# Edge counting: GpSimd forms the node one-hot of every second edge tile

## The chip, the core and the metric

The kernel runs on one core of one Trainium2 chip. The core has TensorE (matrix products and transposes, results in PSUM), VectorE, ScalarE and GpSimd (elementwise engines), and SyncE, which issues most transfers. Each engine works through its own queue in order; engines wait for each other by semaphores. The metric is the time on the device in microseconds (us), median of the runs.

## The reference, cut to what matters

Four layers on 1250 nodes of 512 features; the source and target node of the 41250 edges come as two integer lists, sorted by target.

```python
edge_index = jnp.stack([src, dst])
deg = jnp.maximum(segment_sum(ones(dst.shape), dst, num_segments=1250), 1.0)
x = x + _L0_gnn_ref(_layernorm(x), L0_gnn_wc, L0_gnn_wn, L0_gnn_bias, edge_index)
x = x + _L0_ffn_ref(_layernorm(x)[None], ...)[0]
x = x + _L1_gnn_ref(_layernorm(x), src, dst, deg, ...)
x = x + _L1_ffn_ref(_layernorm(x)[None], ...)[0]
# in _L0_gnn_ref
sums = segment_sum(beta[dst], src, num_segments=x.shape[0])
# in _L1_gnn_ref
neigh_sum = segment_sum(x[edge_src], edge_dst, num_segments=n)
```

The kernel does not gather rows. It first counts the edges into a dense matrix of 1280 by 1280 numbers (and its transpose), how many edges lead from node s to node d, and both graph layers multiply by it. The change is in that counting, `count_edges`.

## The kernel before, in words

The program is a row of stages, each with its own semaphores and a barrier at its end: loading constants (`load_consts`), `count_edges`, the first graph layer, causal attention with the experts, the second graph layer, and the top-16 attention layer.

`count_edges` takes the edges in tiles of 128, ET = 323 of them. Edge e lies on partition e of its tile. A source node s is split into a block `s >> 7` (0 to 9) and a place in the block `s & 127`. For each tile two one-hot matrices are formed, each by one `tensor_scalar` that compares `m.ruler` (0, 1, 2, ... in f16) with a number of its own on each partition (a column of `ends`, f32):

- `hot_b` (128 columns): a one at the source's place in its block;
- `hot_m` (320 columns): a one at (target less the first target of the tile's window) x 10 + block. Since the edges are sorted by target, a tile's targets lie in a window of 32.

TensorE multiplies `hot_b` (as the weights it loads) by `hot_m`, which adds the tile's 128 edges to the counts in PSUM. The counts lie in 25 chunks of 51 targets; a tile whose window crosses a chunk's edge takes two matmuls (`spans`). Four PSUM banks take the chunks in turn. TensorE opens a bank with a product by zero (L327), closes it with another (L330), ScalarE copies it to `m.AT` (L396), and after every third or so chunk TensorE flips a block of 128 targets by ten transposes (L336), which ScalarE writes to `m.A` (L400).

Both one-hots have a ring of HOTS = 8 buffers. In the loop of VectorE (L319 to L322) tile t waits, from t = 8 on, until TensorE has used tile t - 8 (`s_used`), then writes `hot_b` (L305) and `hot_m` (L306); the second counts `s_onehot` up. TensorE waits for `s_onehot` at t + 1 (L376), loads and multiplies (L378) and counts `s_used` up (L382). GpSimd has two small instructions at the stage's start (L256, L257) and then stands at the barrier. The order of each queue is that of the code.

There is a second way through the stage (L310 to L317 and L355 to L368), for edges whose targets do not fit the windows. It is chosen by a flag from the data; with these inputs it is not taken.

Later stages that the prediction reads: `node_rows` (L404 to L428), in which VectorE casts each row block to f16 (`hi`, L422) and GpSimd forms the rest (`lo`, L428), and the causal attention, in which VectorE and GpSimd both scale softmax rows by a number on each partition: VectorE `ex_big` (L1006), GpSimd `ex_small` (L742). In that stage GpSimd also splits keys and queries (L725 to L735).

Of the kernel before, what the change touches and what calls it, by code (L numbers as in the profile page):

```python
# [16 lines left out]
ALU = mybir.AluOpType  # L17
# [3 lines left out]
P = 128  # L21
N = 1250
NT = (N + P - 1) // P
# [8 lines left out]
ET = (NE + P - 1) // P  # L32
EG = (ET + P - 1) // P
HOTS = 8
CD = 51
CHUNKS = 4
WIN = 32
# [150 lines left out]
def window(t):  # L188

    return min(max((t * SLOPE >> 6) - REACH, 0), N - WIN)  # L190


def count_edges(nc, m, io, ahead):
# [4 lines left out]
    def spans(t):  # L198

        lo, hi = window(t), window(t) + WIN  # L200
        return [(c, max(lo, c * CD), min(hi, (c + 1) * CD)) for c in range(lo // CD, (hi - 1) // CD + 1)]
# [7 lines left out]
    def whole(c):  # L209

        return [j for j in range(NT) if c == min((min((j + 1) * P, N) - 1) // CD, NC - 1)]

    with ExitStack() as ctx:
        s = Stage(nc, m, ctx, "ce")
        (s_blank, s_edges, s_tiles, s_base, s_split, s_flag, s_turned, s_cols, s_lined, s_flagged, s_onehot, s_used,
         s_closed, s_drained, s_flipped, s_kept, s_shift) = s.signals(
            "blank edges tiles base split flag turned cols lined flagged onehot used closed drained flipped kept "
            "shift")
        raw = s.sb("raw", [P, 2, EG, P], I32)
        part = s.sb("part", [P, 2, EG, P], I32)  # L220
# [1 line left out]
        ends = s.sb("ends", [P, 3, EG * P])  # L222
        hot_b = s.sb("hot_b", [P, HOTS, P], F16)
# [3 lines left out]
        base = s.sb("base", [P, EG])  # L227
        worst = s.sb("worst", [P, 3])
        flag = s.sb("flag", [1, 2])
# [24 lines left out]
        @block.gpsimd  # L254
        def _(pool):
            pool.iota(tile_i[:, :], [[P, EG]], base=0, channel_multiplier=1).then_inc(s_tiles, 1)  # L256
            pool.memset(m.AT[:, :, NC * CD:NP], 0.0).then_inc(s_tiles, 1)  # L257

        @block.vector
        def _(dve):  # L260
            dve.memset(raw[:, 0, :, :], AWAY).then_inc(s_blank, 1)
            dve.memset(raw[:, 1, :, :], N - 1).then_inc(s_blank, 1)
            dve.memset(none[:, :], 0.0).then_inc(s_blank, 1)

            dve.wait_ge(s_tiles, 1)
            dve.tensor_scalar(tile_i[:, :], tile_i[:, :], SLOPE, None, ALU.mult).then_inc(s_base, 1)
            dve.wait_ge(s_base, 1)
            dve.tensor_scalar(tile_i[:, :], tile_i[:, :], 6, None, ALU.arith_shift_right).then_inc(s_base, 1)
            dve.wait_ge(s_base, 2)
            dve.tensor_scalar(base[:, :], tile_i[:, :], float(-REACH), 0.0, ALU.add, ALU.max).then_inc(s_base, 1)  # L270
            dve.wait_ge(s_base, 3)
            dve.tensor_scalar(base[:, :], base[:, :], float(N - WIN), None, ALU.min).then_inc(s_base, 1)

            dve.wait_ge(s_edges, 16 * 2 * (EG + 1))
            dve.tensor_scalar(part[:, 0, :, :], raw[:, 0, :, :], P - 1, None, ALU.bitwise_and).then_inc(s_split, 1)
            dve.tensor_scalar(part[:, 1, :, :], raw[:, 0, :, :], 7, None, ALU.arith_shift_right).then_inc(s_split, 1)
            dve.wait_ge(s_base, 4)
            dve.tensor_tensor(key[:, 3, :, :], raw[:, 1, :, :], base[:, :].unsqueeze(2).broadcast_to([P, EG, P]),
                              ALU.subtract).then_inc(s_split, 1)
            dve.wait_ge(s_split, 3)  # L280
            dve.tensor_copy(key[:, 0, :, :], part[:, 0, :, :]).then_inc(s_split, 1)
            dve.scalar_tensor_tensor(out=key[:, 1, :, :], in0=key[:, 3, :, :], scalar=float(NT), in1=part[:, 1, :, :],
                                     op0=ALU.mult, op1=ALU.add).then_inc(s_split, 1)
            dve.scalar_tensor_tensor(out=key[:, 2, :, :], in0=raw[:, 1, :, :], scalar=float(NT), in1=part[:, 1, :, :],
                                     op0=ALU.mult, op1=ALU.add).then_inc(s_split, 1)

            drel = key[:, 3, :, :].rearrange("p g e -> p (g e)")
            dve.tensor_reduce(worst[:, 0:1], drel, AX_X, ALU.max).then_inc(s_flag, 1)
            dve.tensor_reduce(worst[:, 1:2], drel, AX_X, ALU.min, negate=True).then_inc(s_flag, 1)
            dve.wait_ge(s_flag, 2)  # L290
            dve.scalar_tensor_tensor(out=worst[:, 2:3], in0=worst[:, 0:1], scalar=float(1 - WIN), in1=worst[:, 1:2],
                                     op0=ALU.add, op1=ALU.max).then_inc(s_flag, 1)
            dve.wait_ge(s_lined, 1)
            dve.tensor_reduce(flag[:, 0:1], ps_w[:, 0:P], AX_X, ALU.max).then_inc(s_flag, 1)
            dve.wait_ge(s_flag, 4)
            dve.tensor_scalar(flag[:, 1:2], flag[:, 0:1], 0.0, None, ALU.is_gt).then_inc(s_flag, 1)
            dve.wait_ge(s_flag, 5)
            dve.tensor_copy(flag_i[:, :], flag[:, 1:2]).then_inc(s_flagged, 1)
            dve.wait_ge(s_turned, 1)
            dve.tensor_copy(ends[:, :, :].rearrange("p n e -> p (n e)"), ps_f[:, 0:3 * EG * P]).then_inc(s_cols, 1)  # L300
            dve.wait_ge(s_cols, 1)
            dve.wait_ge(s_flagged, 1)

            def one_hot(u, b_of, m_of, width):
                dve.tensor_scalar(hot_b[:, u, :], m.ruler[:, 0:P], b_of, None, ALU.is_equal)  # L305
                dve.tensor_scalar(hot_m[:, u, 0:width], m.ruler[:, 0:width], m_of, None, ALU.is_equal  # L306
                                  ).then_inc(s_onehot, 1)

            scattered = dve.value_load(flag_i[0:1, 0:1], min_val=0, max_val=1)
            with dve.If(scattered):  # L310
                with dve.Fori(0, NC) as c:
                    with dve.Fori(0, ET) as t:
                        dve.wait_ge(s_used, c * ET + t + 1)
                        one_hot(0, ends[:, 0, bass.ds(t, 1)], ends[:, 2, bass.ds(t, 1)], CW)
                    dve.wait_ge(s_used, c * ET + ET + 1)
                    dve.tensor_scalar(ends[:, 2, :], ends[:, 2, :], float(-CW), None, ALU.add).then_inc(s_shift, 1)
                    dve.wait_ge(s_shift, c + 1)  # L317
            with dve.Else():
                for t in range(ET):  # L319
                    if t >= HOTS:  # L320
                        dve.wait_ge(s_used, t - HOTS + 2)
                    one_hot(t % HOTS, ends[:, 0, t:t + 1], ends[:, 1, t:t + 1], WIN * NT)  # L322

        @block.tensor
        def _(pe):
            def open_chunk(bank):
                pe.matmul(bank[:, 0:CW], none[:, :], m.ruler[:, 0:CW], start=True, stop=False)  # L327

            def close_chunk(bank):
                pe.matmul(bank[:, 0:CW], none[:, :], m.ruler[:, 0:CW], start=False, stop=True).then_inc(s_closed, 1)  # L330
# [38 lines left out]
            with pe.Else():  # L369
                for t in range(ET):  # L370
                    for c, lo, hi in spans(t):
                        if opens[c] == t:
                            if c >= CHUNKS:
                                pe.wait_ge(s_drained, c - CHUNKS + 1)
                            open_chunk(ps_c[:, c % CHUNKS, :])
                    pe.wait_ge(s_onehot, t + 1)  # L376
                    for c, lo, hi in spans(t):
                        mm = pe.matmul(ps_c[:, c % CHUNKS, (lo - c * CD) * NT:(hi - c * CD) * NT],  # L378
                                       hot_b[:, t % HOTS, :],
                                       hot_m[:, t % HOTS, (lo - window(t)) * NT:(hi - window(t)) * NT],  # L380
                                       start=False, stop=False)
                    mm.then_inc(s_used, 1)  # L382
                    for c, lo, hi in spans(t):
                        if closes[c] == t:
                            close_chunk(ps_c[:, c % CHUNKS, :])
                    for c in range(NC):
                        if closes[c] == t - LATER or (t == ET - 1 and t - LATER < closes[c]):
                            for j in whole(c):
                                pe.wait_ge(s_drained, c + 1)
                                flip(j)  # L390
# [1888 lines left out]
```

## Time and profile before

| | |
|---|---|
| median of 3 runs | 1774.48 us (1774.18 to 1774.99) |
| profiled execution's own time | 1774.77 us |
| its span | 1772.1 us |
| TensorE busy | 1527.8 us (86%) |
| VectorE busy | 1062.0 us (60%) |
| GpSimd busy | 525.6 us (30%) |
| edge tiles 8 to 322, on the timeline | 43.15 to 161.35 us |

The times in the trace are microseconds from the start of the span, in one profiled execution. In the rows PE is TensorE's matmuls, PEld its weight loads, DVE is VectorE, ACT ScalarE, POOL GpSimd, SPq SyncE's queue. An instruction's duration runs from its start to its end; on one engine the next may start before it ends, so the sum of durations can be more than the time that passed. A row of the timeline that ends in x3 merges three instructions in a row.

### The profile page before, as it was taken

The numbers are of one execution on the slowest core, as the hardware profiler recorded it, in microseconds if no ns is written. First come the engines' busy times: TensorE is split into PE (matmuls) and PEld (weight loads), VectorE is DVE, ScalarE is ACT, GpSimd is POOL, SyncE is SP. The second block draws the span as 40 slices with busy tenths as digits, with TensorE's granted clock in tenths as the row PEclk, the third lists the DMA queues.
The fourth block names the chain that finished last, engine by engine and source line by source line (L and its number), as shares of the span: only waits on it lengthen the run. The fifth ranks groups of instructions, "written<-read, shape, count | busy, mean of one in ns | idle before, by whom it ended". The sixth has DMA issues, their size and how long they took to land. (4 is left out here: it accounts for less than half of the span.)

```text
span 1772.1 us, 22747 instructions
## 1 busy us (share of the span) xinstructions
PE 1527.8 (86%) x8385; PEld 940.5 (53%) x8385; DVE 1062.0 (60%) x2052; ACT 699.6 (39%) x1333; POOL 525.6 (30%) x388
## 2 busy tenths in 40 slices
PE   1885888789787788999999989958898999998878
PEld 0332544344466665445454654535586676776654
DVE  4998433333478774111322331574999999999991
ACT  0224000133365554110111132042778778878771
POOL 0001100000456651000000006001876766676550
PEclk9998899899899999999999999989999999999999
DMA  6000100000622212300000020002011011111001
GB/s 220 1 1 1 74 0 0 0 1 1 179 60 43 48 31 86 132 0 0 1 0 0 1 72 0 0 1 60 1 31 31 1 31 31 23 32 31 1 1 58
DMA packets 28570, 56.99 MB, mean 32 GB/s; under 512 B 7904, under 2 KB 12644, under 8 KB 28208
## 3 DMA queue, kind: packets, MB, share of 16 engines
q1 hardware_dynamic: 27600, 54.01, 11.0%
q10 hardware_dynamic: 864, 1.57, 0.3%
q8 instruction: 66, 1.08, 0.3%
q14 instruction: 40, 0.33, 0.1%
HBM read 28.77 MB, written 5.84 MB: 20 GB/s over the span
## 5 line engine op out<-in xcount | busy, mean ns | idle before, releaser
L1431 POOL TENSOR_TENSOR tl_ex<-tl_ex,tl_left 128x1250 f32<-128x1250 f32 x80 | 209.8, 2622 | 37.3 <-ACT tl_left L1733 33.2
L1552 PE MATMUL tl_banks<-identf,tl_ex 128*128 128x128 f32 x800 | 139.4, 290 | 42.2 <-ACT tl_pt L1754 25.7
L1272 DVE SCALAR_TENSOR_TENSOR X<-ex_ps_x,g,X 128x512 f32<-128x512 f32 x80 | 59.9, 750 | 192.6 <-PE ex_ps_x L1165 192.6
L1138 PE MATMUL ex_ps_h<-yt,w 128*128 128x512 f32 (+1 forms) x384 | 144.5, 531 | 0.0
L1165 PE MATMUL ex_ps_x<-w,hid 128*128 128x512 f32 (+1 forms) x320 | 143.1, 599 | 0.0
L1552 PEld LDWEIGHTS tl_banks<-identf,tl_ex 128*128 128x128 f32 x800 | 90.0, 144 | 97.4 <-ACT tl_pt L1754 44.4
L1754 ACT COPY tl_pt<-tl_banks 128x512 f32<-128x512 f32 (+1 forms) x200 | 108.4, 542 | 83.5 <-PE tl_banks L1552 79.7
L1218 ACT ACTIVATE hid<-ex_ps_h,b 128x512 f32<-128x512 f32 (+1 forms) x48 | 29.2, 610 | 242.6 <-PE ex_ps_h L1138 242.6
L1829 DVE MAX8 tl_m<-tl_banks 128x8 f32<-128x1250 f32 x80 | 116.3, 1454 | 5.6 <-PE tl_banks L1529 5.6
L1733 ACT ACTIVATE tl_left<-tl_left,tl_negm 128x1250 f32<-128x1250 f32 x80 | 107.6, 1345 | 29.0 <-DVE tl_left L1837 28.6
L1835 DVE MAX8 tl_m<-tl_left 128x8 f32<-128x1250 f32 x80 | 117.1, 1464 | 2.8
L1905 POOL TENSOR_TENSOR lo<-xn,hi 128x512 f16<-128x512 f32 x5 | 5.9, 1188 | 379.7 <-ACT hi L1995 379.7
L1833 DVE MATCH_REPLACE8 tl_left<-tl_m,tl_banks 128x1250 f32<-128x1250 f32 x80 | 116.0, 1450 | 0.0
L1837 DVE MATCH_REPLACE8 tl_left<-tl_m,tl_left 128x1250 f32<-128x1250 f32 x80 | 115.6, 1445 | 0.0
L378 PE MATMUL ce_ps_c<-ce_hot_m,ce_hot_b 128*128 128x320 f16 (+29 forms) x518 | 98.2, 261 | 14.5
L1138 PEld LDWEIGHTS ex_ps_h<-yt,w 128*128 128x128 f32 x384 | 74.8, 196 | 66.2 <-issue 66.0
L1727 ACT ACTIVATE tl_ex<-tl_banks,tl_negm 128x1250 f32<-128x1250 f32 x80 | 104.9, 1311 | 2.4 <-DVE tl_left L1833 1.3
L1567 PE MATMUL tl_banks<-tl_pt,tl_V 128*64 128x128 f32 x1600 | 104.8, 278 | 0.0
L1165 PEld LDWEIGHTS ex_ps_x<-w,hid 128*128 128x128 f32 (+1 forms) x320 | 60.3, 189 | 73.9 <-issue 73.9
L306 DVE TENSOR_SCALAR ce_hot_m<-ruler,ce_ends 128x320 f16<-128x320 f16 x323 | 96.5, 299 | 0.0
L1567 PEld LDWEIGHTS tl_banks<-tl_pt,tl_V 128*64 128x64 f32 x1600 | 85.7, 137 | 14.2 <-issue 14.2
L1486 PE MATMUL tl_banks<-tl_ct,tl_wt 128*128 128x512 f32 (+1 forms) x192 | 82.0, 554 | 9.2 <-DVE tl_ct L1804 6.2
(268 smaller groups left out, 2963.8 us busy)
## 6 DMA issues: line engine op xcount, KB each, us to landing
kl<-KT SPq DMA_DIRECT2D x16, 320.0 KB, 4.4
qs<-QO SPq DMA_DIRECT2D x16, 320.0 KB, 5.8
tl_kl<-tl_KT SPq DMA_DIRECT2D x16, 320.0 KB, 4.4
tl_qs<-tl_QO SPq DMA_DIRECT2D x16, 320.0 KB, 6.0
w<-in_L_ffn_W SPq DMA_DIRECT2D x8, 512.0 KB
w<-in_L_ffn_W SPq DMA_DIRECT2D x4, 1024.0 KB, 9.8
at_kept<-AT SPq DMA_DIRECT2D x1, 3200.0 KB, 9.0
AT<-at_kept SPq DMA_DIRECT2D x1, 3200.0 KB, 18.9
```

What stands on the lines that cost most here:

```text
L1138: mm = pe.matmul(h_bank(u)[:, 0:w], w1[e][:, k, j * P:(j + 1) * P], yt[:, G % 2, k, 0:w], start=(k == 0), stop=(k == KD - 1))
L1165: mm = pe.matmul(x_bank(v)[0:rows(t), :], hid[:, (EX * G + e) % HIDS, j, r * P:r * P + rows(t)], w2[:, 2 * e + j, :], start=(j == 0), stop ...
L1431: pool.tensor_tensor(ex[:, n % EXS, 0:N], ex[:, n % EXS, 0:N], left[:, n % LEFT, :], ALU.subtract).then_inc(s_probs, 1)
L1552: mm = pe.transpose(ps_t[:, b * P:(b + 1) * P], ex[:, n % EXS, a + b * P:a + (b + 1) * P], m.identf[:, :])
L1567: mm = pe.matmul(ps_o[u * DH:(u + 1) * DH, 0:P], V[:, h // 2 % 2, k, h % 2 * DH:(h % 2 + 1) * DH], pt[:, (2 * j + u) % PTS, k * P:(k + 1) ...
L1727: act.activation(ex[:, n % EXS, 0:N], logits(n)[:, 0:N], ACT.Exp, bias=negm[:, n:n + 1]).then_inc(s_exp, 1)
L1733: act.activation(lf, lf, ACT.Exp, bias=negm[:, n:n + 1]).then_inc(s_rest, 1)
L1754: act.copy(pt[:, n % PTS, a:a + w], ps_t[:, 0:w]).then_inc(s_kept, 1)
L1829: dve.max(m8[:, n % TOPS, 0:8], logits(n)[:, 0:N]).then_inc(s_max, 1)
L1833: dve.match_replace(lf, m8[:, n % TOPS, 0:8], logits(n)[:, 0:N], TAKEN).then_inc(s_read, 1)
L1835: dve.max(m8[:, n % TOPS, 8:16], lf).then_inc(s_max2, 1)
L1837: dve.match_replace(lf, m8[:, n % TOPS, 8:16], lf, TAKEN).then_inc(s_topped, 1)
```

## The change

In the windowed way, GpSimd forms `hot_b` of the odd tiles (1, 3, ..., 321: 161 of them), with the same comparison. It starts when `ends` is there (`s_cols`), waits from tile 9 on for TensorE's use of tile t - 8, as VectorE does, and counts a semaphore of its own up, `s_half_hot`. VectorE forms `hot_b` of even tiles only, and `hot_m` of all. TensorE waits at odd tiles for `s_half_hot` too.

```diff
@@ gpsimd
             pool.memset(m.AT[:, :, NC * CD:NP], 0.0).then_inc(s_tiles, 1)
+            pool.wait_ge(s_cols, 1)
+            for t in range(1, ET, 2):
+                if t >= HOTS:
+                    pool.wait_ge(s_used, t - HOTS + 2)
+                pool.tensor_scalar(hot_b[:, t % HOTS, :], m.ruler[:, 0:P], ends[:, 0, t:t + 1], None, ALU.is_equal
+                                   ).then_inc(s_half_hot, 1)
@@ vector
             def one_hot(u, b_of, m_of, width):
-                dve.tensor_scalar(hot_b[:, u, :], m.ruler[:, 0:P], b_of, None, ALU.is_equal)
+                if b_of is not None:
+                    dve.tensor_scalar(hot_b[:, u, :], m.ruler[:, 0:P], b_of, None, ALU.is_equal)
                 dve.tensor_scalar(hot_m[:, u, 0:width], m.ruler[:, 0:width], m_of, None, ALU.is_equal
                                   ).then_inc(s_onehot, 1)
@@
-                    one_hot(t % HOTS, ends[:, 0, t:t + 1], ends[:, 1, t:t + 1], WIN * NT)
+                    one_hot(t % HOTS, None if t % 2 else ends[:, 0, t:t + 1], ends[:, 1, t:t + 1], WIN * NT)
@@ tensor
                     pe.wait_ge(s_onehot, t + 1)
+                    if t % 2:
+                        pe.wait_ge(s_half_hot, t // 2 + 1)
                     for c, lo, hi in spans(t):
```

VectorE's queue where the ring of eight is full for the first time, tiles 7 to 9, before:

```order
L305 TENSOR_SCALAR ce_hot_b<-ruler,ce_ends 128x128
L306 TENSOR_SCALAR ce_hot_m<-ruler,ce_ends 128x320
L305 TENSOR_SCALAR ce_hot_b<-ruler,ce_ends 128x128 [waits ce2_used]
L306 TENSOR_SCALAR ce_hot_m<-ruler,ce_ends 128x320
L305 TENSOR_SCALAR ce_hot_b<-ruler,ce_ends 128x128 [waits ce2_used]
L306 TENSOR_SCALAR ce_hot_m<-ruler,ce_ends 128x320
```

The same place in the changed kernel, tiles 6 to 9 (its lines stand seven further down):

```order
L312 TENSOR_SCALAR ce_hot_b<-ruler,ce_ends 128x128
L313 TENSOR_SCALAR ce_hot_m<-ruler,ce_ends 128x320 x2
L312 TENSOR_SCALAR ce_hot_b<-ruler,ce_ends 128x128 [waits ce2_used]
L313 TENSOR_SCALAR ce_hot_m<-ruler,ce_ends 128x320
L313 TENSOR_SCALAR ce_hot_m<-ruler,ce_ends 128x320 [waits ce2_used]
```

The `hot_b` of tiles 7 and 9 are gone from VectorE's queue, and the wait on `s_used` of tile 9 is now that of its `hot_m`. GpSimd's queue from the stage's start to the next stages, before:

```order
L256 IOTA ce_tile_i 128x3
L257 MEMSET AT 128x10x5
L213 UNCONDITIONAL_BRANCH
L75 ISA [waits barrier_Pool_Activation_PE_DVE_SP_gather] x2
L424 UNCONDITIONAL_BRANCH
L428 TENSOR_TENSOR gp_lo<-gl_xn,gp_hi 128x512 [waits ce2_edges] x10
```

And in the changed kernel:

```order
L256 IOTA ce_tile_i 128x3
L257 MEMSET AT 128x10x5
L262 TENSOR_SCALAR ce_hot_b<-ruler,ce_ends 128x128 [waits ce2_cols]
L262 TENSOR_SCALAR ce_hot_b<-ruler,ce_ends 128x128 x3
L262 TENSOR_SCALAR ce_hot_b<-ruler,ce_ends 128x128 [waits ce2_used] x157
L213 UNCONDITIONAL_BRANCH
```

161 instructions stand between GpSimd's small ones and the stage's end, 157 of them behind a wait on `s_used`.

## Rows read from the trace of the kernel before

**Rows 1.** The page: span, then busy time and share of each engine.

```profile
span 1772.1 us, 22747 instructions
PE 1527.8 (86%) x8385; PEld 940.5 (53%) x8385; DVE 1062.0 (60%) x2052; ACT 699.6 (39%) x1333; POOL 525.6 (30%) x388
```

**Rows 2.** Table of stretches, tiles 8 to 322: busy us (x instructions), TensorE clock, DMA.

```profile
core 0: us, PE busy (x) PEld busy (x) DVE busy (x) ACT busy (x) POOL busy (x), PEclk, DMA share, GB/s
43.15:161.35 118.20, 103.76 (x652) 42.27 (x650) 118.20 (x630) 25.62 (x41) 0.00 (x0) 1.00 0.01 1
```

**Rows 3.** Waits, 43.1 to 161.4: total us, times, longest.

```profile
PEld ce_ps_c L378 <- DVE ce_hot_m L306: 73.9, 283, 0.3
...
DVE ce_hot_b L305 <- PE ce_ps_c L378: 3.9, 1, 3.9
```

**Rows 4.** Groups by line of VectorE (busy us, mean ns), then timeline (start, us).

```profile
L306 DVE TENSOR_SCALAR ce_hot_m<-ruler,ce_ends 128x320 f16<-128x320 f16 x315 | 94.1, 299 | 0.0
L305 DVE TENSOR_SCALAR ce_hot_b<-ruler,ce_ends 128x128 f16<-128x128 f16 x315 | 78.6, 250 | 3.9 <-PE ce_ps_c L378 3.9
...
50.29 0.25 DVE L305 TENSOR_SCALAR ce_hot_b<-ruler,ce_ends 128x128 f16<-128x128 f16 x1
...
50.45 0.30 DVE L306 TENSOR_SCALAR ce_hot_m<-ruler,ce_ends 128x320 f16<-128x320 f16 x1
50.66 0.25 DVE L305 TENSOR_SCALAR ce_hot_b<-ruler,ce_ends 128x128 f16<-128x128 f16 x1
```

**Rows 5.** Timeline of the stage's start, VectorE and TensorE.

```profile
36.16 0.25 DVE L305 TENSOR_SCALAR ce_hot_b<-ruler,ce_ends 128x128 f16<-128x128 f16 x1 [1.19 <-issue]
...
42.24 0.60 PE L327 MATMUL ce_ps_c<-ruler,ce_none 128*128 128x510 f16 x1 [7.06 <-issue]
...
42.64 2.60 PE L378 MATMUL ce_ps_c<-ce_hot_m,ce_hot_b 128*128 128x320 f16 x9
...
43.15 0.26 DVE L305 TENSOR_SCALAR ce_hot_b<-ruler,ce_ends 128x128 f16<-128x128 f16 x1 [3.90 <-PE ce_ps_c L378]
```

**Rows 6.** Timeline of TensorE around a flip.

```profile
122.19 0.60 PEld L336 LDWEIGHTS ce_ps_f<-ident,AT 128*128 128x128 f16 x10
...
122.75 0.19 PEld L378 LDWEIGHTS ce_ps_c<-ce_hot_m,ce_hot_b 128*128 128x128 f16 x2
...
123.22 0.17 PEld L378 LDWEIGHTS ce_ps_c<-ce_hot_m,ce_hot_b 128*128 128x128 f16 x2 [0.18 <-DVE ce_hot_m L306]
```

**Rows 7.** Groups by line of GpSimd, whole span: busy us, mean ns.

```profile
L742 POOL TENSOR_SCALAR ex_small<-ex_small,inv 128x128 f32<-128x128 f32 x8 | 4.8, 605 | 41.9 <-DVE inv L1001 41.9
L742 POOL TENSOR_SCALAR ex_small<-ex_small,inv 128x256 f32<-128x256 f32 x8 | 7.4, 923 | 6.4 <-DVE inv L1001 5.4 <-POOL kl L727 1.0
L742 POOL TENSOR_SCALAR ex_small<-ex_small,inv 128x640 f32<-128x640 f32 x8 | 15.1, 1883 | 20.1 <-DVE inv L1001 20.1
L1425 POOL TENSOR_SCALAR tl_negm<-tl_m 128x1 f32<-128x1 f32 x80 | 16.8, 210 | 118.0 <-DVE tl_m L1829 101.5 <-ACT tl_left L1733 14.7
L1409 POOL CAST tl_kh<-tl_kl 128x1280 fp32r<-128x1280 f32 x7 | 8.8, 1251 | 0.5
L126 POOL TENSOR_SCALAR_AFFINE_SELECT identf<-identf 128x128 f32<-128x128 f32 x1 | 0.3, 292 | 0.2 <-POOL ld_ruler_i L124 0.2
```

**Rows 8.** Timeline of `node_rows`: VectorE's casts and GpSimd's subtractions, single instructions.

```profile
169.05 0.43 DVE L422 CAST gp_hi<-gl_xn 128x512 f16<-128x512 f32 x1 [1.45 <-ACT gl_xn L415]
169.57 1.15 POOL L428 TENSOR_TENSOR gp_lo<-gl_xn,gp_hi 128x512 f16<-128x512 f32 x1 [146.21 <-DVE gp_hi L422]
170.93 0.41 DVE L422 CAST gp_hi<-gl_xn 128x512 f16<-128x512 f32 x1
172.31 1.34 POOL L428 TENSOR_TENSOR gp_lo<-gl_xn,gp_hi 128x512 f16<-128x512 f32 x1
172.56 1.38 DVE L422 CAST gp_hi<-gl_xn 128x512 f16<-128x512 f32 x1
173.61 1.33 POOL L428 TENSOR_TENSOR gp_lo<-gl_xn,gp_hi 128x512 f16<-128x512 f32 x1
173.85 1.37 DVE L422 CAST gp_hi<-gl_xn 128x512 f16<-128x512 f32 x1
174.90 1.33 POOL L428 TENSOR_TENSOR gp_lo<-gl_xn,gp_hi 128x512 f16<-128x512 f32 x1
```

**Rows 9.** Timeline of causal attention: VectorE's L1006 and GpSimd's instructions beside it.

```profile
468.82 0.87 DVE L1006 TENSOR_SCALAR ex_big<-ex_big,inv 128x1250 f32<-128x1250 f32 x1
473.09 0.62 POOL L742 TENSOR_SCALAR ex_small<-ex_small,inv 128x128 f32<-128x128 f32 x1 [9.26 <-DVE inv L1001]
473.78 1.25 POOL L725 CAST kh<-kl 128x1280 fp32r<-128x1280 f32 x1
474.40 1.24 DVE L1006 TENSOR_SCALAR ex_big<-ex_big,inv 128x1152 f32<-128x1152 f32 x1
479.94 1.25 POOL L730 CAST qh<-qs 64x1280 fp32r<-64x1280 f32 x1
480.16 1.57 DVE L1006 TENSOR_SCALAR ex_big<-ex_big,inv 128x1024 f32<-128x1024 f32 x1
```

More of the change, by code:

```diff
@@ L214, in count_edges @@
         s = Stage(nc, m, ctx, "ce")
-        (s_blank, s_edges, s_tiles, s_base, s_split, s_flag, s_turned, s_cols, s_lined, s_flagged, s_onehot, s_used,
+        (s_blank, s_edges, s_tiles, s_base, s_split, s_flag, s_turned, s_cols, s_lined, s_flagged, s_onehot, s_half_hot, s_used,
          s_closed, s_drained, s_flipped, s_kept, s_shift) = s.signals(
-            "blank edges tiles base split flag turned cols lined flagged onehot used closed drained flipped kept "
+            "blank edges tiles base split flag turned cols lined flagged onehot half_hot used closed drained flipped kept "
             "shift")
```

## The prediction

> **What bounds the kernel now.** The page says that VectorE is busy 60% of the span and GpSimd 30%, and that the profiled execution's span is 1772.1 us; its own time is 1774.77 us, so 2.7 us lie around the span, and the median of the three runs shown is 1774.48 us, 0.3 us below it [rows 1]. The shares are averages; the change touches one stage, so I read that stage alone. The table of stretches from 43.15 to 161.35 us has VectorE busy all 118.20 us with 630 instructions, GpSimd at 0.00 and TensorE's granted clock at 1.00, its upper level of 2.4 GHz [rows 2]. The view of waits over the same stretch says who is late: TensorE's weight load waits for `ce_hot_m` 283 times, 73.9 us in all, while VectorE waits once, 3.9 us, and that just ahead of the stretch [rows 3]. VectorE sets the pace and TensorE follows tile by tile.
>
> The 630 instructions are 315 tiles (8 to 322) of two each, so a tile costs 118.20 / 315 = 0.375 us. That is less than the sum of the durations, 0.250 + 0.299 us: the timeline has the start of `hot_m` 0.16 us after that of `hot_b`, and the next `hot_b` starts 0.21 to 0.22 us after `hot_m`, before `hot_m` has ended [rows 4]. What an instruction costs VectorE in this row is the spacing, not the duration: 0.163 us for `hot_b`, 0.212 for `hot_m`. The first eight tiles are outside this: VectorE builds them from 36.16 us on, in 3 us, and TensorE cannot take the first before 42.24 us [rows 5]. After the last tile comes a tail of banks, copies and a flip that does not change, and then a stage boundary. Nothing else runs beside this stage for later use except loads that are over by about 44 us, so each us more or less here is one at the end.
>
> **How much room TensorE has.** It waits 73.9 of 118.2 us, which leaves (118.2 - 73.9) / 315 = 0.14 us of its own per tile. After ten transposes (0.60 us) it takes up two tiles with 0.19 us of loads between them, opens a bank and is back to waiting at 123.22 us [rows 6]. TensorE is no bound at any pace discussed here; even at its lower clock level, where I double all of it, it would want 0.28 us of the tile. The new wait of TensorE on `s_half_hot` at odd tiles stands just behind one on `s_onehot` and costs nothing as long as GpSimd is ahead; behind it are only that tile's matmuls.
>
> **Removed.** 161 instructions `hot_b` leave VectorE; 4 of them belong to the first eight tiles and are hidden behind TensorE's late start, 157 count (tiles 9, 11, ..., 321). Each gives back its spacing: 157 x 0.163 = -25.6 us. A pair of tiles then costs VectorE 0.750 - 0.163 = 0.587 us. Nothing else is late before that: TensorE needs 0.28 us a pair.
>
> **Added: GpSimd's own pace.** GpSimd runs 161 `TENSOR_SCALAR` of 128x128 f16 with a per-partition scalar. The trace has no such instruction in f16. The nearest is the softmax scaling at L742, the same operation, 128x128 in f32 with a per-partition scalar: 605 ns. From there to 640 columns (1883 ns) it grows by 1278 / 512 = 2.50 ns a column, and with one column it takes 210 ns (L1425). Lower bound: the rate of GpSimd's CAST, 1251 ns for 1280 columns, or 0.98 ns a column: 210 + 127 x 0.98 = 335 ns. Upper bound: the same operation at twice the columns, 923 ns, in case the comparison or the 16-bit type doubles the work of a column [rows 7]. I take 605 ns, since operation, shape and the kind of scalar agree and only type and comparison do not. Two instructions of GpSimd in a row leave about 0.07 us between them (0.62 us from 473.09, the next at 473.78 [rows 9]). So GpSimd alone would need 0.675 us for each pair, less than the 0.750 of now. GpSimd's waits on `s_used` come true eight tiles ahead of need, and nothing else is in its queue until the stage ends.
>
> The Trainium skill, in "GPSIMD Engine Reference", section "4.1 Engine selection", calls one-input work on GpSimd roughly line rate. The row of L742 disagrees at 2.50 ns a column, the row of CAST is close to it; the sum by that rule is that of the first rival below.
>
> **Added: what GpSimd does to VectorE.** This decides. The stage has never had both engines at work, but two later ones have. In the stage that splits the node rows, VectorE casts 128x512 f32 to f16 while GpSimd subtracts. With GpSimd idle the cast takes 0.43 or 0.41 us; beside GpSimd it takes 1.37 to 1.38. It ends about 0.29 us after GpSimd's instruction has ended (172.31 + 1.34 = 173.65; 172.56 + 1.38 = 173.94) and GpSimd's next one takes 1.33 us instead of 1.15. One of each goes by every 1.30 us (172.31, 173.61, 174.90) [rows 8]. They exclude each other and take turns. A second place shows it for the very kind of instruction at stake: VectorE's `TENSOR_SCALAR` with a per-partition scalar (L1006) takes 0.87 us for 1250 columns with GpSimd idle; beside a GpSimd CAST that runs until 475.03 us, 1152 columns take 1.24 us and end 0.61 us after it; beside one until 481.19, 1024 columns take 1.57 us and end 0.54 us after it [rows 9]. Both are 0.53 ns a column with no start left over, so the instruction stood ready and its data moved only once GpSimd was done.
>
> Does that hold for `hot_b` and `hot_m`? From 128 to 320 columns they grow by 299 - 250 = 49 ns, 0.26 ns a column [rows 4], twice the rate of the blocked L1006, so I expect them to want at least as much of what is shared. The Trainium skill says it outright in "SBUF — State Buffer", section "Who interferes with whom": VectorE's copies, casts and tensor_scalars in the two-port modes, of which the four-a-cycle one is the fastest, and GpSimd lock each other out for a whole instruction. By that rule the trace agrees for the casts and L1006 [rows 8, 9]; no row here shows it for f16 on both sides.
>
> The price of one GpSimd instruction to VectorE: GpSimd hides some of its start. Of a 1.30 us turn 0.29 is VectorE's, so GpSimd keeps the way for 1.01 of the 1.15 us that it takes alone, 0.14 less [rows 8]. For ours: 0.605 - 0.14 = 0.46 us. VectorE's next instruction has its own start behind it by then: alone 1152 columns would take about 0.82 us (0.87 less 98 columns of 0.53 ns), and after the release they took 0.61, so 0.21 is hidden [rows 9]; the cast hid 0.41 - 0.29 = 0.12 [rows 8]. A `hot_m` of 0.30 us then ends 0.09 to 0.18 us after the release, where it would have ended 0.21 us after its forerunner. Price: 0.46 + 0.09 - 0.21 = 0.34 us, or 0.43 with the cast's figure. I take 0.34, as L1006 is the same operation.
>
> **Sum.** A pair goes from 0.750 to 0.587 + 0.34 = 0.927 us. 157 x 0.34 = +53.4, less 25.6, is +27.8 us. Against the profiled execution 1774.8 + 27.8 = 1802.6, against the median **1802.3 us**. The rest (157 waits on GpSimd, 161 on TensorE) is in queues that have slack: 0.
>
> **Rivals.**
> (1) *The short instruction*, faster. GpSimd forms the one-hot at its CAST's rate, 0.335 us. It keeps the way 0.195 us, the price is 0.195 + 0.09 - 0.21 = 0.075 and the net -0.088 us a pair: 157 x -0.088 = -13.8, 1760.7 us. The point from which it decides is a price of 0.163, that is an instruction of about 0.42 us (0.163 + 0.21 - 0.09 + 0.14). For it: CAST and AFFINE_SELECT (292 ns for 128x128). Against it: all eight L742 of 128x128 average 605 [rows 7]. Chance 0.09, and 0.04 for a length close to the point, within 0.2%.
> (2) *No exclusion* at this rate. Then GpSimd's own 0.675 us is the pair: -0.075 x 157 = -11.8, 1762.7 us. Against it rows 8 and 9. Chance 0.05.
> (3) *The long instruction*: 0.923 us. It keeps the way 0.78, the price is 0.66 and the net +0.50: +78, 1852.6 us. Chance 0.12.
> (4) *VectorE keeps GpSimd out* until it has run eight tiles ahead and stalls on `s_used`; then four GpSimd instructions run alone (2.7 us) after VectorE's burst (2.35), with a hand-over through TensorE of some 0.5 us each way (its first matmul starts at 42.64, VectorE resumes at 43.15 [rows 5]): 6.05 us for four pairs, 1.51 a pair, +119 us, 1894 us. Against it: the turns of rows 8, where GpSimd got its turn although VectorE's next cast was already waiting. Chance 0.04.
>
> **How the numbers follow.** My own case (a price between 0.20 and 0.60) has 0.66. About 0.2% or 3.5 us is what a measurement of this kernel can tell from no change. Faster is (1) and (2), 0.14; same 0.04; slower 0.66 + 0.12 + 0.04 = 0.82. The range goes from 1770, under the low prices, to 1853, case (3); it leaves out (1), (2) and (4), 0.18.
>
> **What would show it.** In the changed profile: GpSimd's new line of 161 instructions at 0.6 to 0.75 us; `hot_m` no longer all at 0.299 us, but one in two or three near 0.6 to 0.75 us; the stage 28 us longer (about 0.93 us from one GpSimd instruction to the next); TensorE still waiting for `ce_hot_m`, or for `ce_hot_b` of GpSimd; all later stages the same length. I am wrong in the price if the instructions on GpSimd last under 0.42 us, in the exclusion if `hot_m` keeps its 0.299 us, and in the turns if GpSimd's instructions come in clusters of four.

## The result, and the profile after

The changed kernel takes 1768.0 us (median of 15 runs, 1762.67 to 1773.66), the kernel before 1775.32 us in the same rounds (15 runs, 1772.44 to 1780.06). The ratio is 0.9953 with a 95% interval of 0.9941 to 0.9965: 7 to 8 us, or 0.5%, faster. Timed again on another occasion the ratio was 0.9965 (0.9948 to 0.9982). The forecast was 28 us slower. One execution of a version further down is left out of its ratio: it ran at a granted clock of 0.558 instead of about 0.96 and took 2600.35 us.

The page of the changed kernel, against [rows 1]: the span is 6.7 us shorter, VectorE has 161 instructions fewer, GpSimd 161 more and 113 us more of work.

```profile
span 1765.4 us, 22908 instructions
PE 1508.5 (85%) x8385; PEld 943.1 (53%) x8385; DVE 1054.9 (60%) x1891; ACT 698.9 (40%) x1333; POOL 638.8 (36%) x549
```

The table of stretches of the changed kernel (busy us and instructions of TensorE, its weight loads, VectorE, ScalarE and GpSimd, then TensorE's clock) for 157 pairs of tiles in the loop, against [rows 2]; then the same kernel's groups by line of VectorE and GpSimd there, against [rows 4, 7]:

```profile
42.67:153.24 110.57, 82.30 (x648) 42.89 (x646) 110.57 (x471) 25.60 (x41) 110.48 (x157) 1.00 0.01 1
...
L313 DVE TENSOR_SCALAR ce_hot_m<-ruler,ce_ends 128x320 f16<-128x320 f16 x314 | 95.2, 343 | 0.0
L312 DVE TENSOR_SCALAR ce_hot_b<-ruler,ce_ends 128x128 f16<-128x128 f16 x157 | 42.8, 272 | 0.0
...
L262 POOL TENSOR_SCALAR ce_hot_b<-ruler,ce_ends 128x128 f16<-128x128 f16 x157 | 110.7, 724 | 6.0 <-PE ce_ps_c L387 6.0
```

VectorE's 471 instructions are 157 x 3. A pair takes 110.57 / 157 = 0.704 us, where it took 0.750. Both engines are busy all the time, and `hot_m` has grown from 299 to 343 ns on average. The waits of the same kernel, from 43 to 160 us, against [rows 3]:

```profile
PEld ce_ps_c L387 <- DVE ce_hot_m L313: 58.6, 134, 0.6
PE ce_ps_c L387 <- DVE ce_hot_m L313: 21.2, 64, 0.4
...
PE ce_ps_c L387 <- POOL ce_hot_b L262: 0.6, 4, 0.2
```

TensorE still waits for the one-hots, as forecast, and has time to spare. VectorE's last `hot_m` ends at 153.24 us, before at 161.43, 8.2 us earlier; 7.1 of it is the loop (118.1 us from the `hot_m` of tile 8 on before, 111.0 now) and 1.1 is that TensorE began a little earlier in this execution. The rest of the program took 1610.67 us before and 1612.16 us now, in which nothing was changed; 1.5 us is well within what runs of one kernel differ by.

So VectorE gave back what was forecast and GpSimd took less than forecast. Of 0.587 us a pair without `hot_b`, 0.704 - 0.587 = **0.117 us** is the price of one GpSimd instruction, where the prediction had 0.34 and the point that decides lay at 0.163.

The timeline shows the price instruction by instruction (start, duration, both in us). First the stage's beginning, where GpSimd was not held up, then the steady loop, in which the pattern repeats every two pairs:

```profile
34.01 2.39 POOL L262 TENSOR_SCALAR ce_hot_b<-ruler,ce_ends 128x128 f16<-128x128 f16 x4 [11.68 <-DVE ce_ends L306]
...
35.80 0.60 POOL L262 TENSOR_SCALAR ce_hot_b<-ruler,ce_ends 128x128 f16<-128x128 f16 x1
...
35.84 0.37 DVE L312 TENSOR_SCALAR ce_hot_b<-ruler,ce_ends 128x128 f16<-128x128 f16 x1
36.13 0.37 DVE L313 TENSOR_SCALAR ce_hot_m<-ruler,ce_ends 128x320 f16<-128x320 f16 x1
...
80.38 0.85 POOL L262 TENSOR_SCALAR ce_hot_b<-ruler,ce_ends 128x128 f16<-128x128 f16 x1
...
80.76 0.27 DVE L312 TENSOR_SCALAR ce_hot_b<-ruler,ce_ends 128x128 f16<-128x128 f16 x1
80.95 0.37 DVE L313 TENSOR_SCALAR ce_hot_m<-ruler,ce_ends 128x320 f16<-128x320 f16 x1
...
81.20 0.60 POOL L262 TENSOR_SCALAR ce_hot_b<-ruler,ce_ends 128x128 f16<-128x128 f16 x1
81.24 0.42 DVE L313 TENSOR_SCALAR ce_hot_m<-ruler,ce_ends 128x320 f16<-128x320 f16 x1
...
81.78 0.85 POOL L262 TENSOR_SCALAR ce_hot_b<-ruler,ce_ends 128x128 f16<-128x128 f16 x1
```

Undisturbed, GpSimd's instruction lasts 0.60 us, the 605 ns that was taken from L742, and four of them in a row take 2.39 us, 0.60 each with nothing between them. In the loop every second one lasts 0.85: there GpSimd is held up and VectorE runs its pair in its own 0.59 us. Beside the end of that one and the next, of 0.60, VectorE is held up, and its two `hot_m` last 0.37 and 0.42. VectorE starts its pairs at 80.17, 80.76, 81.58, 82.17: 0.59, 0.82, 0.59. The rows from 35.80 on already contradict the forecast's picture: a `hot_b` ends at 36.21 while GpSimd is busy until 36.40. VectorE is held up, but not until GpSimd is done.

### The profile page after: what moved, and what is told of

Same layout as the page of the kernel before. It is cut to its first block and busy times, and to the rows that moved or that the text cites. A ratio compares the mean times of both kernels' runs of the same rounds, so it can differ in the third digit from the quotient of the medians.

```text
span 1765.4 us, 22908 instructions
## 1 busy us (share of the span) xinstructions
PE 1508.5 (85%) x8385; PEld 943.1 (53%) x8385; DVE 1054.9 (60%) x1891; ACT 698.9 (40%) x1333; POOL 638.8 (36%) x549
## 3 DMA queue, kind: packets, MB, share of 16 engines
q10 hardware_dynamic: 864, 1.57, 0.3%
## 5 line engine op out<-in xcount | busy, mean ns | idle before, releaser
L262 POOL TENSOR_SCALAR ce_hot_b<-ruler,ce_ends 128x128 f16<-128x128 f16 x161 | 113.1, 722 | 17.7 <-DVE ce_ends L306 11.7
L387 PE MATMUL ce_ps_c<-ce_hot_m,ce_hot_b 128*128 128x320 f16 (+29 forms) x518 | 75.0, 252 | 28.3 <-DVE ce_hot_m L313 21.2
```

The source lines that it names most:

```text
L262: pool.tensor_scalar(hot_b[:, t % HOTS, :], m.ruler[:, 0:P], ends[:, 0, t:t + 1], None, ALU.is_equal).then_inc(s_half_hot, 1)
```

## The experiments

Two theories of the price were put against each other. **W**, the prediction's: GpSimd keeps VectorE out for its whole duration less 0.14 us. **P**: it keeps VectorE out only during a part of its instruction. The measure throughout is the loop, from VectorE's start on the `hot_m` of tile 8 to the end of its last `hot_m`: 118.1 us in the kernel before. The loops are read from one profiled execution of each kernel.

### Spare instructions on GpSimd beside an unchanged VectorE

Four kernels add to the kernel before a row of comparisons on GpSimd into a buffer that nobody reads. VectorE's work is that of before, so the loop's growth over their number is the price. The first of them:

```diff
+            pool.wait_ge(s_cols, 1)
+            pool.wait_ge(s_used, 16)
+            for i in range(140):
+                if i >= 4:
+                    pool.wait_ge(s_idle, i - 3)
+                pool.tensor_scalar(spare[:, i % 4, :], m.ruler[:, 0:P], ends[:, 0, i:i + 1], None, ALU.is_equal
+                                   ).then_inc(s_idle, 1)
```

The others have f32 input and output (x2), 50 instructions of 512 columns in f16 (x3), and 50 of 512 in f32 (x4).

> The kernel before, with 140 more instructions on GpSimd beside VectorE's one-hot loop: the same comparison, 128x128 f16 with a per-partition scalar, into a spare buffer nobody reads, from tile 16 on. VectorE's own work is untouched, so the lengthening of the loop divided by 140 is the price of one such instruction to VectorE. Theory W (the prediction's: GpSimd keeps VectorE out for its whole duration less 0.14 us): 0.34 us each, the loop 48 us longer. Theory P (it keeps the shared way for only a part of its duration): 0.10 to 0.20 us each, 14 to 28 us longer.

> The same with f32 input and output, 128x128. Theory W: 0.34 us each, 48 us in all, as in f16. Theory P, if the part that GpSimd holds goes by bytes: twice the price of the f16 run, 0.2 to 0.4 us. Theory P, if it goes by columns or instructions: the price of the f16 run.

> 50 spare GpSimd instructions of 128x512 f16 instead of 140 of 128x128. At 2.5 ns a column one lasts 1.56 us. Theory W: 1.56 - 0.14 - 0.12 = 1.3 us each, the loop 65 us longer, and no hot_m or hot_b ends in the middle of a GpSimd instruction. Theory P: VectorE's instructions go on ending while GpSimd's runs; the price is 0.2 to 0.6 us, 10 to 30 us in all.

> The same 50 with f32 input and output, 128x512, which is the very form of L742 beside L1006 in the attention stage, where L1006 ended only after GpSimd had. Theory W: 65 us longer. Theory P with a part that goes by bytes: twice the f16 run. If this one shows full exclusion and the f16 one does not, the type decides; if neither does, the length of VectorE's instructions decides (short ones slip in between).

| spare instructions | loop, us | price, us | mean duration on GpSimd |
|---|---|---|---|
| 140 of 128 columns, f16 | 136.2 | 18.1 / 140 = 0.13 | 0.874 |
| 140 of 128 columns, f32 | 152.3 | 34.2 / 140 = 0.24 | 0.639 |
| 50 of 512 columns, f16 | 157.6 | 39.5 / 50 = 0.79 | 1.576 |
| 50 of 512 columns, f32 | 157.5 | 39.4 / 50 = 0.79 | 1.574 |

W had 0.34 and 1.3: it falls in all four. The 512-column run shows why. Groups by line of GpSimd in that run, then its timeline:

```profile
L264 POOL TENSOR_SCALAR ce_spare<-ruler,ce_ends 128x512 f16<-128x512 f16 x50 | 77.8, 1576 | 23.3 <-PE ce_ps_c L385 23.3
...
79.91 1.56 POOL L264 TENSOR_SCALAR ce_spare<-ruler,ce_ends 128x512 f16<-128x512 f16 x1
79.95 0.69 DVE L312 TENSOR_SCALAR ce_hot_b<-ruler,ce_ends 128x128 f16<-128x128 f16 x1
80.56 0.29 DVE L313 TENSOR_SCALAR ce_hot_m<-ruler,ce_ends 128x320 f16<-128x320 f16 x1
80.77 0.24 DVE L312 TENSOR_SCALAR ce_hot_b<-ruler,ce_ends 128x128 f16<-128x128 f16 x1
80.94 0.64 DVE L313 TENSOR_SCALAR ce_hot_m<-ruler,ce_ends 128x320 f16<-128x320 f16 x1
81.46 1.57 POOL L264 TENSOR_SCALAR ce_spare<-ruler,ce_ends 128x512 f16<-128x512 f16 x1
```

Beside one GpSimd instruction of 1.56 us VectorE runs four. The first is lengthened by 0.44 us (0.69 against 0.25), the next two not at all, the fourth by 0.34 (0.64 against 0.30). GpSimd's comparison shuts VectorE out twice, once in its first half and once before its end, and leaves it alone between. The two stretches make up 0.79 of 1.57 us. P holds. P's size for 512 columns (0.2 to 0.6) was too low. Bytes do not matter at 512 columns, where f16 and f32 cost the same. That run's expectation had said that, if neither type showed full exclusion, the length of VectorE's instructions would decide. The copy below, beside the same short instructions, and two rows of the kernel before, shown with the account of the prediction, speak against it: the operation on GpSimd matters, and where in it VectorE's instruction falls.

At 128 columns f32 costs twice f16, but bytes alone are not the reason: with f32, GpSimd lasts 0.64 us, nearly undisturbed, and VectorE pays 0.24; with f16, GpSimd lasts 0.87 and VectorE pays 0.13; and further down f16 comparisons at GpSimd's undisturbed pace cost VectorE about 0.2. The two engines share out the delay in different ways, depending on how their instructions fall together; most of each run is one repeating pattern. What makes it settle into this one or that is open.

### Do other instructions keep VectorE out all the time?

The prediction's price was read beside a subtraction (its 0.14 us) and beside casts. So here is a copy of 512 columns on GpSimd, then a memset, which reads nothing; each takes the place of the 512-column comparison, 100 times instead of 50, with an f32 buffer:

```diff
-                pool.tensor_scalar(spare[:, i % 2, :], m.ruler[:, 0:512], ends[:, 0, i:i + 1], None, ALU.is_equal
+                pool.tensor_copy(spare[:, i % 2, :], m.bias0[:, :]
                                    ).then_inc(s_idle, 1)
```

```diff
+                pool.memset(spare[:, i % 2, :], 1.0
```

> The kernel before with 100 spare GpSimd copies of 128x512 f32, about 0.71 us each at 0.98 ns a column. If GpSimd keeps VectorE out while it reads and while it writes (0.43 us each for 512 columns), and a copy does both at once without a pause between, the price is near the whole of its duration: 0.40 to 0.60 us each, 0.6 to 0.8 of the duration, against 0.50 of it for the 512-column comparisons. If instead the price is a fixed share of the duration whatever the operation, it is 0.36 us.

> The kernel before with 100 spare GpSimd memsets of 128x512 f32, which read nothing. If the two stretches in which a 512-column comparison keeps VectorE out (0.45 and 0.35 us) are its reading and its writing, a memset has one of them: one lengthened VectorE instruction for each memset, about 0.3 to 0.4 us, the loop 30 to 40 us longer. If the two stretches are two halves of one job of another kind, a memset shows two or none.

The copy: loop 159.7 us, 41.6 / 100 = 0.42 us each, 0.63 of its 0.66 us, as P expected for an operation without a pause. Its timeline:

```profile
80.34 0.63 DVE L312 TENSOR_SCALAR ce_hot_b<-ruler,ce_ends 128x128 f16<-128x128 f16 x1
80.88 0.66 POOL L264 COPY ce_spare<-bias 128x512 f32<-128x512 f32 x1
80.89 0.74 DVE L313 TENSOR_SCALAR ce_hot_m<-ruler,ce_ends 128x320 f16<-128x320 f16 x1
81.55 0.64 DVE L312 TENSOR_SCALAR ce_hot_b<-ruler,ce_ends 128x128 f16<-128x128 f16 x1
```

One VectorE instruction for each copy, every one of them lengthened: here the engines take strict turns, as in [rows 8]. The prediction's way of reckoning is right for copies: 0.66 - 0.14 + 0.09 - 0.21 = 0.40 us against 0.42 measured. It is the comparison that leaves a gap.

The memset: loop 140.2 us, 22.1 / 100 = 0.22 us each, less than the 0.30 to 0.40 expected. Its timeline:

```profile
79.61 3.02 POOL L264 MEMSET ce_spare<- 128x512 f32 x5
...
80.31 0.59 DVE L312 TENSOR_SCALAR ce_hot_b<-ruler,ce_ends 128x128 f16<-128x128 f16 x1
...
80.46 0.52 DVE L313 TENSOR_SCALAR ce_hot_m<-ruler,ce_ends 128x320 f16<-128x320 f16 x1
...
80.90 0.59 DVE L312 TENSOR_SCALAR ce_hot_b<-ruler,ce_ends 128x128 f16<-128x128 f16 x1
```

A memset comes by every 0.60 us and two VectorE instructions with it. The `hot_b` ends at 80.90 and the `hot_m` 0.08 us later, at 80.98; the next `hot_b` ends at 81.49. So there is one stop for each memset, which holds up two instructions already under way, against two stops for a comparison of the same width. That fits the reading that the two stretches of a comparison are its reading and its writing, but its 0.22 us is less than either of them (0.44 and 0.34). It does not prove it: no run had reading alone.

### Who sets the pace of 0.704 us?

In the changed kernel both engines are busy without a gap. Would GpSimd need 0.704 us a pair by itself? This run takes `hot_m` of the odd tiles away from VectorE; an odd tile uses the `hot_m` of the tile before, so the counts are others. VectorE's part of the edit (TensorE's waits and its reading of `hot_m` follow suit):

```diff
-                for t in range(ET):
+                for t in range(0, ET, 2):
                     if t >= HOTS:
-                        dve.wait_ge(s_used, t - HOTS + 2)
-                    one_hot(t % HOTS, None if t % 2 else ends[:, 0, t:t + 1], ends[:, 1, t:t + 1], WIN * NT)
+                        dve.wait_ge(s_used, t - HOTS + 3)
+                    one_hot(t % HOTS, ends[:, 0, t:t + 1], ends[:, 1, t:t + 1], WIN * NT)
```

> The changed kernel without hot_m of the odd tiles: VectorE forms hot_b and hot_m of even tiles only, and an odd tile's matmuls read the hot_m of the tile before (the counts are therefore others). VectorE then needs 0.375 us a pair and TensorE 0.28, so GpSimd alone is left to set the pace. If GpSimd's own pace is its undisturbed 0.585 us a pair and the changed kernel's 0.705 came from the two engines disturbing each other, the pair falls to 0.59 to 0.65 us and the loop is 92 to 102 us long. If 0.705 is what GpSimd needs by itself once it waits for TensorE, it stays at 0.705 and the loop at 111 us.

The table of stretches of that run for its loop:

```profile
42.67:135.17 92.50, 79.68 (x649) 43.77 (x647) 88.82 (x316) 25.61 (x41) 92.37 (x157) 1.00 0.01 1
```

GpSimd is busy throughout and needs 92.37 / 157 = 0.588 us a pair, about its undisturbed pace (0.60 at the stage's start). The loop is 92.5 us. Both lie at the low end of what was expected. So 0.704 is nobody's own pace. Alone, GpSimd would need 0.58 to 0.60 us a pair and VectorE 0.587; side by side in the changed kernel each holds the other up by about 0.12 us.

The same row shows more. VectorE's two instructions a pair would take 0.375 us by their spacings, yet it is busy 88.82 of 92.50 us, or 0.57 us a pair: it pays about 0.2 us for each GpSimd instruction, and GpSimd pays next to nothing. The price of the very same f16 comparison is thus 0.117 us in the changed kernel and about 0.2 here, on either side of the 0.163 that decides whether the change pays.

### GpSimd every third tile, ScalarE instead of GpSimd

```diff
-            for t in range(1, ET, 2):
+            for t in range(2, ET, 3):
```

(VectorE's and TensorE's conditions change from `t % 2` to `t % 3 == 2`.)

> The changed kernel with GpSimd forming hot_b of every third tile instead of every second. VectorE gives up 0.163 us per three tiles and pays 0.12 to 0.24 for one GpSimd instruction, so three tiles cost 1.08 to 1.20 us against 1.125 before: the loop 113 to 126 us, the kernel 5 us faster to 8 us slower than before. GpSimd has time to spare here, so if the price stays 0.12 the gain is two thirds of the change's; if the price depends on how the two engines fall together, it moves.

Loop 115.2 us, ratio 0.9982 (0.9963 to 1.0002): no change that can be told. Three tiles take 115.2 / 105 = 1.10 us, so the price is 1.10 - 0.962 = 0.13 us, about that of the change, for fewer `hot_b` saved. GpSimd had slack, waiting 29.0 us for TensorE between 45 and 150 us, and the price did not fall: it does not come from GpSimd being short of time.

ScalarE has not delayed VectorE in any row read here. It can form the same matrix in two instructions (in GpSimd's place):

```diff
+                    act.activation(away[:, k % 4, :], m.ruler[:, 0:P], ACT.Abs, bias=less[:, t:t + 1]).then_inc(s_away, 1)
+                    act.wait_ge(s_away, k + 1)
+                    act.activation(hot_b[:, t % HOTS, :], away[:, k % 4, :], ACT.Relu, bias=m.ones[:, 0:1], scale=-1.0
+                                   ).then_inc(s_half_hot, 1)
```

`less` is `ends` with the sign turned. Ahead of the copy of chunk c these stand for the tiles up to seven beyond the chunk's last.

> Every third hot_b is formed by ScalarE instead of GpSimd, as Relu(1 - Abs(ruler - b)) in two instructions, exact for these integers; GpSimd is idle. If what eats the change's gain is the way that GpSimd and VectorE share, the price here is 0: hot_m stays at 0.299 us, three tiles cost 0.962 us, the loop is 101 us long and the kernel 17 us faster than before. If any third engine that reads and writes on-chip memory beside VectorE delays it, hot_m grows here too. A risk of its own: ScalarE also copies the banks out (0.59 us) and writes m.A (1.24 us), and may then be late with a hot_b, which would show as TensorE waiting for it; that can give back up to 10 us.

> ScalarE forms every fourth hot_b instead of every third. In the run with every third, VectorE kept its 0.299 us but the loop was 107.0 us instead of the 101.1 that its spacings give, since ScalarE was late after a copy of m.A. With every fourth, four tiles cost VectorE 1.500 - 0.163 = 1.337 us, 105.3 us in all. If ScalarE's lateness is gone, the loop is 105 to 106 us and the kernel 12 to 13 us faster than before; if it stays, 108 to 110 us.

> The changed kernel itself, timed beside the ScalarE version on one chip. Its loop was 111.0 us against 118.1: 0.9953 of the time before, 0.994 to 0.997 expected.

> The version with ScalarE forming every fourth hot_b, once more, beside the changed kernel. Its loop was 105.4 us, 12.7 below that of before and 5.6 below the changed kernel's: 0.992 to 0.994 of the time before expected. If its interval lies below the changed kernel's, it beats both.

Groups by line in the loop of the run with every third:

```profile
L310 DVE TENSOR_SCALAR ce_hot_m<-ruler,ce_ends 128x320 f16<-128x320 f16 x315 | 84.9, 297 | 4.2 <-PE ce_ps_c L384 4.2
L309 DVE TENSOR_SCALAR ce_hot_b<-ruler,ce_ends 128x128 f16<-128x128 f16 x210 | 52.2, 248 | 4.7 <-PE ce_ps_c L384 4.5
...
L411 ACT ACTIVATE ce_hot_b<-ce_away,ones 128x128 f16<-128x128 f16 x105 | 42.2, 402 | 3.4
```

`hot_m` keeps its 0.297 us: ScalarE beside it costs VectorE nothing, GpSimd does. The loop was 107.0 us, not 101, and the waits of that run say why:

```profile
PE ce_ps_c L384 <- ACT ce_hot_b L411: 11.1, 13, 1.5
```

TensorE waits for a late `hot_b` of ScalarE (11.1 us in 13 waits), and VectorE in turn 4.7 us for TensorE. Each of these waits of over 1 us comes after ScalarE has written a block of `m.A` (1.24 us), the shorter ones after a copy of a bank (0.57 us). With every fourth tile the loop is 105.4 us, the 105.3 that VectorE's spacings give.

| kernel | loop, us | ratio to before (95% interval) | median, us |
|---|---|---|---|
| the change | 111.0 | 0.9953 (0.9941 to 0.9965) | 1768.0 |
| the change, again | 111.1 | 0.9965 (0.9948 to 0.9982) | 1768.45 |
| ScalarE, every third | 107.0 | 0.9922 (0.9897 to 0.9947) | 1762.35 |
| ScalarE, every fourth | 105.4 | 0.9936 (0.9909 to 0.9962) | 1762.97 |
| ScalarE, every fourth, again | 105.4 | 0.9939 (0.9919 to 0.9959) | 1762.57 |

All ScalarE versions are faster than the kernel before. Their loops are 4 to 6 us shorter than the change's and their medians about 6 us lower; the intervals of the whole kernel still overlap with the change's, for every fourth tile also where both were timed together (the rows marked again). The last run's expectation had asked for an interval below the changed kernel's; that they beat the change rests on the loop, and the times alone do not show it.

## Why the prediction was wrong, point by point

**What bounds the loop**: right before the change. VectorE's spacings, 0.163 and 0.212 us, carried every sum, and the run with ScalarE at every fourth tile met them within 0.1 us in 105. TensorE had room, as said.

**Removed, -25.6 us**: right. With ScalarE in GpSimd's place 0.163 us per `hot_b` came back, where ScalarE kept up.

**GpSimd's instruction, 605 ns**: right, 0.60 us undisturbed. The 0.07 us between two of them was not there; it was read where GpSimd waits for an instruction of its own in between.

**GpSimd and VectorE exclude each other, for f16 on both sides too**: right. `hot_m` grew, and rival (2) falls. That is also what the Trainium skill says in "SBUF — State Buffer", section "Who interferes with whom"; but it says that the one to issue first has the shared ports for the whole instruction, and the timeline of the 512-column run has two VectorE instructions run at full speed in the middle of a GpSimd comparison of 1.56 us. For copies the rule and the trace agree, for comparisons they do not.

**The price, 0.34 us**: the step that failed. "GpSimd keeps the way for 1.01 of the 1.15 us that it takes alone, 0.14 less [rows 8]. For ours: 0.605 - 0.14 = 0.46 us." The rule came from a subtraction and from casts, which keep VectorE out throughout, and was carried over to an operation at 2.5 ns a column against a cast's 0.98. That difference stood in [rows 7] and could have been a hint. A comparison of 512 columns shuts VectorE out for 0.79 of its 1.57 us only; what GpSimd does in the rest is not shown. The price measured 0.117 us, so this term is 157 x 0.117 = +18.4 instead of +53.4 us; with -25.6 the sum is -7.2, and the loop, from which the price was taken, fell by 7.1.

The kernel before already held the counterexample, in the stage that the prediction read: GpSimd's `TENSOR_SCALAR` of 512 columns (L742, a scaling) beside VectorE's L1006 of 768, twice:

```profile
490.10 1.56 POOL L742 TENSOR_SCALAR ex_small<-ex_small,inv 128x512 f32<-128x512 f32 x1 [2.96 <-DVE inv L1001]
491.12 0.95 DVE L1006 TENSOR_SCALAR ex_big<-ex_big,inv 128x768 f32<-128x768 f32 x1
...
657.47 1.82 POOL L742 TENSOR_SCALAR ex_small<-ex_small,inv 128x512 f32<-128x512 f32 x1 [4.86 <-DVE inv L1001]
...
658.20 0.62 DVE L1006 TENSOR_SCALAR ex_big<-ex_big,inv 128x768 f32<-128x768 f32 x1
```

The first L1006 starts 1.02 us after GpSimd's instruction and ends 0.41 us after it, as W has it, or a stretch shut out at the end. The second starts 0.73 us after, takes the 0.62 us that 768 columns need alone (0.87 less 482 columns of 0.53 ns) and is over while GpSimd still runs; here it is GpSimd that lasts 0.26 us longer. Of eight such meetings in this trace seven look like the first and one like the second.

**The sign** hung on this term alone. The point that decides, 0.163 us, was right, but rival (1) reached it only by a GpSimd instruction of 0.42 us. The duration undisturbed stayed at 0.60; the part of it in which VectorE is shut out was the small one. That case, between full exclusion and none, was missing among the rivals. Nor does a lower price follow from the missing case alone: the same comparison cost about 0.2 us in the run without the odd `hot_m`. Why the changed kernel fell into the cheap pattern is open. The range stopped at 1770 us, just above the 1768.0 measured.

**What would show it**: `hot_m` "near 0.6 to 0.75 us" was wrong (at most 0.42), "TensorE still waiting for `ce_hot_m`" right, and GpSimd's clusters of four, rival (4), did not come.

## What to carry to other kernels

How long one engine shuts another out is not its instruction's duration: take it from rows of the same operation, all of them, and look at where in it the other's instruction falls. An operation that takes far more time for each column than a copy may leave gaps in which the other runs, as the comparison does here. If part of the work of the engine that sets the pace is moved to one that holds it up, count the price for each instruction against the spacing that it saves; here 0.117 against 0.163 us left under a third of the gain. An engine that did not hold it up (here ScalarE, at every fourth tile) shortened the loop more with half as many instructions moved.

## What the runs showed of the hardware that I had not expected

- A GpSimd comparison of 512 columns (1.56 us) stops VectorE's f16 one-hots in two stretches of 0.44 and 0.34 us with a free one between; a copy of 512 columns (0.66 us) lets one VectorE instruction through for each copy; a memset (about 0.6 us) stops VectorE once.
- A 128-column comparison cost VectorE 0.12, 0.13 or about 0.2 us in f16 and 0.24 in f32, while it lasted 0.72, 0.87, 0.62 and 0.64 us itself: the engines fall into a repeating pattern, and who pays differs from one pattern to the next.
- Two engines with undisturbed paces of 0.58 to 0.60 and 0.587 us a pair, both always busy and neither waiting for a semaphore, ran together at 0.704.
